# A four-layer graph network on one core: the loops of all five engines' programs written out, with constants for addresses and waits

## What is computed

```python
x = _layernorm(x + _L0_gnn_ref(x, W, b, src, dst))            # relu(segment_sum(x[src], dst) @ W.T + b)
x = _layernorm(x + _L1_gnn_ref(x, edge_index, edge_attr_2, ...))
#   h = concat(x[row], x[col], edge_attr) @ W1 + b1, batch norm over the edges, relu,
#   msgs = h @ W2 + b2, segment_sum(msgs, row) / (count + 1) + x
x = _layernorm(x + _L2_gnn_ref(x, edge_index, edge_attr_64, ...))
#   q, k, v; k_j = k[src] + e; v_j = v[src] + e; softmax of q[dst] . k_j over each node's edges,
#   conv = weighted sum of v_j + skip + bias; h = ln(conv + x); ln(ffn(h) + h), ffn with gelu, 4 * 128 wide
x = _layernorm(x + _L3_gnn_ref(x, edge_index, ...))
#   projection, leaky_relu of src_score[src] + tgt_score[dst], exp, normalised segment_sum, bias
```

## Time and profile before

| | us |
|---|---|
| median of three runs | 7631.62 (7593.73 to 7636.19) |
| the profiled execution | 7591.09 |
| its span in the profile | 7589.4 |

### The profile page before, as it was taken

The page is one execution under the profiler, slowest core; times in us unless marked ns, Lnnn a source line. Parts: engine busy times, 40 slices in busy tenths (PEclk is TensorE's granted clock), DMA queues, the critical chain, the costliest instruction groups (busy, mean ns, idle before and its releaser), DMA issues. The chain is left out here.

```text
span 7589.4 us, 131785 instructions
## 1 busy us (share of the span) xinstructions
PE 5517.2 (73%) x28275; PEld 3876.3 (51%) x28275; DVE 4490.1 (59%) x15688; ACT 2411.0 (32%) x6375; POOL 4342.3 (57%) x4005
## 2 busy tenths in 40 slices
PE   6777888688856665666677619777777776777788
PEld 4555666444456552222566518633433334666666
DVE  4455766322255557999455449754544445666698
ACT  0002555311111214444111002155555554222255
POOL 5663555555568887888555400145555555555598
PEclk8888999788877877888777759888988887888899
DMA  4554555333356668888555525433433333333466
GB/s 129 167 166 154 171 162 158 114 118 121 119 108 107 106 98 235 263 257 247 158 174 173 153 43 146 130 87 84 96 87 86 82 87 73 73 73 71 104 186 175
DMA packets 1467697, 1013.62 MB, mean 134 GB/s; under 512 B 167328, under 2 KB 1345650, under 8 KB 1467476
## 3 DMA queue, kind: packets, MB, share of 16 engines
q1 hardware_dynamic: 1282276, 737.37, 33.7%
q0 software_dynamic: 163072, 210.16, 14.8%
q10 hardware_dynamic: 22240, 64.90, 2.4%
HBM read 512.60 MB, written 522.48 MB: 136 GB/s over the span
## 5 line engine op out<-in xcount | busy, mean ns | idle before, releaser
L433 POOL DMA_INDIRECT l_nodes_ag<-agg,l_nodes_at x392 | 387.4, 988 | 1097.4 <-ACT l_nodes_at L427 997.8
L2224 PE MATMUL l_nodes_f<-l_nodes_h_t_s,w_f 128*128 128x512 f32 x784 | 487.4, 750 | 320.8 <-ACT l_nodes_act_t L2176 284.9
L1533 POOL DMA_INDIRECT agg<-l_edges_b_rows,l_edges_b_at x392 | 607.5, 1550 | 131.2 <-issue 66.8
L535 POOL DMA_INDIRECT to_col<-l_nodes_col_s,l_nodes_rank_at x392 | 404.3, 1031 | 378.4 <-ACT l_nodes_col_s L1221 274.5
L2402 POOL DMA_INDIRECT l_edges_proj<-proj_tab,l_edges_src_s x392 | 379.7, 969 | 370.6 <-DVE l_edges_src_s L2311 249.2
L1686 PE MATMUL l_nodes_y<-w_qkvs,l_nodes_x_t 128*128 128x512 f32 x784 | 448.9, 726 | 190.4 <-DVE l_nodes_qkvs L1623 171.6
L1772 POOL DMA_INDIRECT l_edges_a_kv<-kv_tab,l_edges_a_src_s x392 | 380.3, 970 | 304.2 <-DVE l_edges_a_src_s L1726 199.9
L1291 POOL DMA_INDIRECT l_edges_a_at_row<-to_row,l_edges_a_row_i x392 | 377.8, 964 | 278.6 <-DVE l_edges_a_row_i L1260 171.6
L497 DVE TENSOR_SCALAR l_edges_a_at_rank<-l_edges_a_keys,own_rank 128x512 f32<-128x512 f32 (+3 forms) x784 | 255.3, 388 | 472.6 <-DMA l_edges_fetched<-in_x,l_edges_index 243.1
L933 POOL DMA_INDIRECT l_edges_fetched<-in_x,l_edges_index x392 | 388.6, 991 | 227.6 <-DVE l_edges_index L906 120.4
L535 POOL DMA_INDIRECT tgt_tab<-l_nodes_ext,l_nodes_rank_at x392 | 393.4, 1003 | 180.4 <-issue 115.0
(11 more groups left out here) (332 smaller groups left out, 14510.7 us busy)
## 6 DMA issues: line engine op xcount, KB each, us to landing
agg<-zeros ACTq DMA_DIRECT2D x98, 516.0 KB
l_nodes_xg<-x SPq DMA_DIRECT2D x196, 256.0 KB
kv_tab<-l_nodes_qkvs SPq DMA_DIRECT2D x98, 512.0 KB
agg<-l_edges_rows SPq DMA_DIRECT2D x98, 266.0 KB
l_nodes_ag<-agg SPq DMA_DIRECT2D x98, 266.0 KB
proj_tab<-l_nodes_ext SPq DMA_DIRECT2D x98, 264.0 KB
l_nodes_ag<-agg SPq DMA_DIRECT2D x98, 258.0 KB
l_nodes_ag_odd<-agg SPq DMA_DIRECT2D x98, 258.0 KB
```

The lines of the kernel that those rows point to most:

```text
L433: pool.indirect_dma_start(ag[k][:, j, :], None, table, bass.IndirectOffsetOnAxis(at[k][:, j:j + 1].bitcast(U32), 0),).then_inc(a_in[k][j], 16)
L535: pool.indirect_dma_start(table, bass.IndirectOffsetOnAxis(at[k][:, j:j + 1].bitcast(U32), 0), rows[:, j, :], None, bounds_check=nodes - 1 ...
L1533: pool.indirect_dma_start(agg1[j // 2], bass.IndirectOffsetOnAxis(at[k][:, j:j + 1].bitcast(U32), 0), rows[k][:, j, :], None, compute_op=A ...
L2224: pe.matmul(f[m % 2][:], w_f1[:, m * P:(m + 1) * P], h_t_s[k][:], start=True, stop=True).then_inc(f_done, 1)
```

## The change

`rotation` and `pipeline` get an argument `loop`, and with `loop=False` the straight part goes on over all groups and the loop is left out. Every call in the file, 49 of them on all five engines, passes `loop=False`. With that, `i` is a number when the program is written, and all addresses and wait counts are constants; the steps, their order, the buffers and the waits themselves stay as they are. What SP reads from the table (`value_load`) is still read at run time. The new file has one line less near its top, so its line numbers are one smaller.

```diff
-def pipeline(eng, pairs, *stages):
+def pipeline(eng, pairs, *stages, loop=True):
 
     most = max(lag for lag, _ in stages)
-    start = 1 + (most + 1) // 2
+    start = 1 + (most + 1) // 2 if loop else pairs
     for n in range(2 * start):
         for lag, step in stages:
             if n >= lag:
                 step(*divmod(n - lag, 2))
-    with eng.Fori(start, pairs) as i:
-        for k in range(2):
-            for lag, step in stages:
-                step(i + (k - lag) // 2, (k - lag) % 2)
+    if loop:
+        with eng.Fori(start, pairs) as i:
+            for k in range(2):
+                for lag, step in stages:
+                    step(i + (k - lag) // 2, (k - lag) % 2)
...
-def rotation(eng, groups, *stages):
+def rotation(eng, groups, *stages, loop=True):
...
-    start = -(-(most + RING) // RING)
+    start = -(-(most + RING) // RING) if loop else -(-(groups + most) // RING)
     whole = max(start, groups // RING)
...
-                        rotation(sp, groups, (0, load), (4, store))
+                        rotation(sp, groups, (0, load), (4, store), loop=False)
                         all_out(sp, h_out)
...
-                        rotation(dve, groups, (6, lambda i, k: balance(dve, i, k)), (2, invert), (3, mix), (8, bias))
+                        rotation(dve, groups, (6, lambda i, k: balance(dve, i, k)), (2, invert), (3, mix), (8, bias), loop=False)
```

## The result

The changed kernel takes 7444.33 us (median of four runs, 7435.54 to 7453.31) against 7633.9 us before (7593.73 to 7638.0): a ratio of 0.9735, 95% interval 0.9699 to 0.9772. That is 190 us, three times the forecast of 62 and just inside the stated range. The direction was right, the size wasn't. The profiled execution has a span of 7451.3 us against 7589.4, 138 us less.

A forecast was written before the change was run, and what follows sets the result against it. POOL's indirect DMAs were taken to pace most stages, PE edges_2b. Terms -12 (nodes_0), -8 (nodes_1), -10 (nodes_3), -18 (nodes_2), -14 (stalls) sum to -62 us: 7529, scaled by 1.0053 to 7569 us; range 7430 to 7685.

The forecast's parts named there:

- The bound of the edge stages: edges_1a, edges_1b, edges_2a, edges_3 and layer 0's gather: POOL's indirect DMA issue sets the pace, so plain removal gives 0 us.
- Stalls: Stages with indirect DMAs: fewer SP register steps may shorten stalls, mostly hidden behind POOL; -14 us, ends 0 and -80.
- Rival B: Whole kernel much faster: nodes_0 -45, stalls -80, nodes_2 -45, nodes_3 -17, nodes_1 -12; -199 us, 7431 us; chance 0.10.
- nodes_2: Stage nodes_2, no engine full: half of the exposed turn ends and waits lies on the path; -18 us, ends 0 and -45.
- nodes_0: Stage nodes_0: a quarter of the scatter pace difference, 1.70 against 1.837 us, is the loop's; -12 us, ends 0 and -45.
- nodes_1: Stage nodes_1: DVE's exposed steps go, but POOL leaves at most 12 us; -8 us, ends 0 and -42.
- nodes_3: Stage nodes_3: exposed steps on handshakes between DVE, POOL and PE go; -10 us, ends 0 and -20.
- edges_2b: Stage edges_2b: PE is the limit and its register operations hide behind streaming matmuls; 0 us.
- edges_1b: Stage edges_1b: POOL's indirect DMAs set the pace and hide the other engines' register operations; 0 us.
- edges_3: Stage edges_3: POOL's indirect DMAs set the pace and hide the other engines' register operations; 0 us.
- Instruction fetch: All engines' longer programs: about 220 packets for PE and 350 for the others, waiting taken as 0 us.
- rival C: Whole kernel slower, engines standing a microsecond or more at regular instruction counts; mild end 7685 us; chance 0.20.

## Why the prediction was wrong, point by point

**The bound of the edge stages.** I wrote that the stages with indirect DMAs are paced by POOL's issuing. On these chips they were not. In the earlier trace rows the 314 DMAs of 520 us need 314 x 1.26 = 395 us, 0.30 included; a quarter of the stretch was idle. I took equal pace in straight and looped code for a limit of POOL, when it was the same stalls in both. The row that should have stopped me is that sum. On the chips without stalls POOL is the bound, 1.28 us a DMA, and there the change is worth nothing in edges_1a, as the step said.

**Stalls: the step that failed.** "Most of it is hidden, since POOL, which sets the pace, goes on issuing meanwhile. I take -14", with ends 0 and -80. The gain by way of the stalls was 108 and 141 us (the two pairs' spans differ by 138 and 171; less the 30 of the chip without stalls), and 160 and 118 by the medians. Two things were wrong in the step. POOL doesn't go on through a stall: in edges_1a it issues the twelve DMAs that it has indices for and then stands with the others, so the stalls weren't hidden but cost the kernel before 1207 us. And the end of -80 was half of one row's 172.1 us, waits of one copy of ACT, where the whole kernel's stalls were to be sized. Rival B had the mechanism in part (stalls and nodes_0), and its 7431 us is near the 7444 measured; that is luck in good part, since it gave 45 us to nodes_2, where 98 and 55 went, 17 to nodes_3, where 4 went, and nothing to edges_3, which took 38 back. Its idea that a stall lasts as long as SP's steps doesn't fit edges_1a, where 32 late copies became 31. Why fewer steps shorten the stalls in nodes_2 and nodes_0 stays open.

**nodes_2**: forecast -18, ends 0 and -45, measured -98 and -55. The plain part that the -18 was meant for is -1 (1081 to 1080; another profile of the full change without stalls has 1075): next to nothing of 0.10 us per wait and 0.44 per turn lay on the path. The gain there is stalls. How the steps of the engines share in it stays open: each engine alone gave 45 to 87 us, though ACT, PE and POOL have no long register step in the whole trace, and idle steps put on SP or DVE took none of it away.

**nodes_0**: forecast -12, measured -43 and -58; without stalls 0. The difference in the earlier trace rows between 1.70 and 1.837 us per scatter was the loop's doing after all, by way of the stalls, as far as the totals show. The changed kernel has 319 in 540 us, 1.69:

```profile
800.00:1340.00 540.00, 339.09 (x319) 0.99 0.62 177
```

**nodes_1**: forecast -8, measured -14, -9 and -11: right, and about the cap of 12 that POOL's 600 of 610 us gave. **nodes_3**: forecast -10, measured -4, -8 and -6; near. (Its "4.27 if a group more is counted" is a slip: 250/59 is 4.24.) DVE alone gave 21 and 22 there, on both kinds of chip (below). **edges_2b**: 0, measured 0. **edges_1b**: 0, measured +4 on both kinds; with PE or SP alone 751 and 749 us, with DVE alone 747 and 745. I have no explanation. **edges_3**: forecast 0, measured +38 and +21 with stalls, -19 without. So the plain steps do lie on its path, and the stalls changed the sign, which no run here explains; DVE alone gives 787 with stalls and 567 without, so the 19 us come from the others.

**Instruction fetch**: 235 and 373 packets came for 220 and 350 forecast, and rival C's +187 us fell: edges_2b, where PE uses them fastest, is unchanged at 378 us, and PE alone written out gained.

**The range** held the result (7430 to 7685), but only because rival B had been let in to its end. Without the stalls the sum of the other steps was -48 for 30 measured.

## What to carry to other kernels

Before calling an engine the bound, multiply its count by its own spacing within a burst and compare with the stretch: a quarter left over is a wait that someone else makes, and equal pace in two versions doesn't prove a limit. When three engines that wait for one signal all go on at the same moment, long after its producer ended, look for what else ended just before that moment. Loops written out with constants are worth little where nothing is disturbed (here 0.5%) and 2.1 to 2.65% where stalls are there to be shortened. Before a run with a loop left in is read as the price of the loop, see in its trace that the branch still goes back. Compare kernels on the same chip only, and profile both there: the same kernel was shorter by 16% on some chips here, far more than by any edit.

## What was not expected of the hardware

While POOL issues indirect DMAs every 1.26 us, some register steps take about 700 ns instead of 40 to 60, of SP from about the third DMA in a row (37 of 163 in nodes_2), of DVE from about the sixth, and of ACT, PE and POOL never. In edges_1a signals of finished work are seen 2 to 11 us late, most of them 2.0 to 2.5 us after the row of DMAs has ended. With 1.85 us between the DMAs (edges_1b) no step is long, and the stage takes 746 us with stalls elsewhere and 745 without. This held on the chips with the kernel before at 7568 to 7634 us, and there was none of it on the two at 6385 and 6388. What differs between them no run here shows.

In nodes_3, DVE alone written out is faster than everything written out: 408.7 and 408.4 us against 425.5, 425.1 and 424.7. The kernel with its loops of one turn is at 411.8 too. DVE's L2549 takes 42.99 us for 62 there and 50.79 for 58 in the full change (the line alone, 250 us of the stage, first DVE alone, then the full change, both on the chip of the table's last columns):

```profile
6010.00:6260.00 250.00, 42.99 (x62) 1.00 0.73 198
```

```profile
6010.00:6260.00 250.00, 50.79 (x58) 1.00 0.69 188
```

The same instruction takes 0.69 us in one order of events and 0.88 in the other, and the kernel before lies between with 46.53 for 58. That the other engines' earlier starts fall on it at a worse moment is a guess. A version with everything written out, but in nodes_3 only DVE, should win some 16 us, an estimate from the two stage times; it wasn't run.
